# A gated cross-attention and expert kernel: another order of the set-up, scores straight from q, a folded gate, and heads gathered by transfers

## The reference

```python
x = x + tanh(g_xattn[0]) * xattn(layernorm(x), ctx, ctx, adj, mask, Wq, bq, Wk, bk, Wv, bv, Wo, bo)
x = x + tanh(g_ffn[0]) * moe(layernorm(x), gate_w, w1, b1, w2, b2)
# xattn: 16 heads of 16; softmax(Q K^T / 4 + adj, shut where mask == 0) V, then Wo and bo
# moe: 8 experts of 256 -> 1024 -> 256 with relu; each token goes to the one expert whose
#      gate logit (x @ gate_w.T) is largest, times its softmax probability
```

## Time and profile before

| | |
|---|---|
| three runs | 552.46, 554.51 (median), 555.67 us |
| profiled execution, span | 548.5 us (its own time is not given apart from the runs) |
| busy: PE, DVE, ACT, POOL | 526.3, 302.3, 309.1, 297.9 us |
| first score, last score | 27.35 us, 361.17 us |
| expert loop | from 413.99 us |
| DMA queue of SP | 46600 packets, 67.72 MB |

### The profile page before, as it was taken

How to read it: one execution, slowest core, us unless ns; L and a number is a source line. 1 busy time by engine, 2 the same in 40 slices (tenths; PEclk the granted TensorE clock), 3 DMA queues, 4 the chain that set the end, 5 groups by cost and what they waited for, 6 DMA issues and landing times. The chain is left out here.

```text
span 548.5 us, 13306 instructions
## 1 busy us (share of the span) xinstructions
PE 526.3 (96%) x4123; PEld 405.1 (74%) x4124; DVE 302.3 (55%) x923; ACT 309.1 (56%) x678; POOL 297.9 (54%) x424
## 2 busy tenths in 40 slices
PE   8999999989999999999999999888999999999997
PEld 5577667667666667666676666658899999999996
DVE  2776587976677887668885878845340211111111
ACT  4366678665678665778675676664332333333322
POOL 5346566665567575468574556555244444443451
PEclk9999999999999999999999999999999999999999
DMA  8633625400405510204520057499136665555570
GB/s 288 206 110 132 192 65 183 149 31 6 150 21 192 166 50 1 79 10 153 180 85 1 11 184 250 147 362 320 59 103 218 211 205 196 178 187 184 189 210 1
DMA packets 51489, 77.67 MB, mean 142 GB/s; under 512 B 9945, under 2 KB 34601, under 8 KB 51305
## 3 DMA queue, kind: packets, MB, share of 16 engines
q1 hardware_dynamic: 46600, 67.72, 37.0%
q0 software_dynamic: 4192, 8.73, 5.0%
q10 hardware_dynamic: 640, 0.52, 0.3%
HBM read 52.76 MB, written 8.35 MB: 111 GB/s over the span
## 5 line engine op out<-in xcount | busy, mean ns | idle before, releaser
L1588 DVE CUSTOM_DVE_ANT_0 prob<-bank,adjm 128x512 f32<-128x512 f32 x256 | 172.3, 688 | 70.6 <-issue 39.9
L1229 ACT ACTIVATE pt<-bank 128x512 f32<-128x512 f32 x256 | 152.1, 596 | 87.7 <-PE bank L951 81.2
L682 POOL TENSOR_SCALAR prob<-prob,negmax 128x512 f32<-128x512 f32 x190 | 132.0, 698 | 117.6 <-DVE negmax L1588 113.4
L951 PE MATMUL bank<-ident,prob 128*128 128x128 f32 x1024 | 154.8, 274 | 2.2 <-POOL prob L682 1.3
L951 PEld LDWEIGHTS bank<-ident,prob 128*128 128x128 f32 x1024 | 124.2, 141 | 39.7 <-issue 13.7
L1299 ACT ACTIVATE adjm<-bank,colsm 128x128 f32<-128x128 f32 x184 | 52.6, 368 | 105.0 <-PE bank L1127 80.0
L940 PE MATMUL bank<-w2s 128*128 128x512 bf16 x256 | 97.5, 381 | 8.5 <-DVE negmax L1588 5.7
L963 PE MATMUL bank<-pt,vals 128*32 128x256 f32 x1024 | 68.3, 385 | 0.9 <-DVE vals L1386 0.5
L1127 PEld LDWEIGHTS bank<-xT,pt 128*128 128x128 f32 x576 | 67.1, 192 | 0.9
L1127 PE MATMUL bank<-xT,pt 128*128 128x128 f32 x576 | 67.2, 275 | 0.0
L1137 PE MATMUL bank<-w2s,adjm 128*128 x288 | 65.1, 379 | 0.0
(11 more groups left out here) (195 smaller groups left out, 624.4 us busy)
## 6 DMA issues: line engine op xcount, KB each, us to landing
pt<-in_L_ffn_w SPq DMA_DIRECT2D x19, 1024.0 KB
w2s<-parts SPq DMA_DIRECT2D x96, 128.0 KB
w2s<-in_L_ffn_w SPq DMA_DIRECT2D x8, 1024.0 KB
maski<-in_mask_Bx1xSxS_ik SPq DMA_DIRECT2D x4, 1024.0 KB, 5.6
w2s<-parts SPq DMA_DIRECT2D x56, 64.0 KB, 2.1
xres<-in_x SPq DMA_DIRECT2D x18, 128.0 KB
x_d<-rows SPq DMA_DIRECT2D x18, 128.0 KB
xn_d<-rows SPq DMA_DIRECT2D x18, 128.0 KB
```

The lines of the kernel that those rows point to most:

```text
L682: po.tensor_scalar(prob[:, m], prob[:, m], -1.0, negmax[:, m:m + 1], ALU.mult, ALU.add).then_inc(s_shpool, 1)
L951: mm = pe.transpose(tr_bank[n % NTB][:, c * P:(c + 1) * P], prob[:, n % TILES % NB, c * P:(c + 1) * P], ident[:])
L1229: act.activation(pt[:, g % 2, :, j, q2 * P:(q2 + 1) * P], tr_bank[c % NTB][:].rearrange("p (c q) -> p c q", c=QT), ACT.Exp).then_inc(s_cac ...
L1588: ve.tensor_tensor_reduce(out=prob[:, m % NB], in0=sc_bank[m % NS][:], in1=adjm[:, qt], scale=-1.0, scalar=BIG, op0=ALU.add, op1=ALU.min, ...
```

## The change

1. Set-up. ScalarE issues Wk and the context; the sync queue x, Wq and small rows, and only one quarter of mask and bias first. k of the first half is projected before x is normalised. The eight tiles of head group 0 (both query tiles) of batch 0 are scored with float32 operands: k in `kf`, and `qm[:, j]`, a copy of q in which the rows of other heads are multiplied by zero (`own`). The group's stack is made later (tile 32 needs it).
2. Gate. Its weights are centred (mean taken off) and folded: Wo gets 8 more columns `Wo^T gate`, the bias 8 more elements, and a new use `gate x` gives x's part from the normalised x, multiplied back by `std`. A logit is then column 256 to 263 of the row, times 1/std, on GpSimd. Uses `normed` and `gate` are gone.
3. Heads. `heads` and `turn` are gone, except in the tail for the last half. Per half batch nine transfers gather `o_sb` into `oc` and the sums into 16 rows of `rc`; VectorE inverts these, four transfers spread them over `rs`, and VectorE multiplies `oc` by `rs` into `atT`.
4. Steps of many uses are moved by a few, and the load of b2 stands later on the sync queue.

```diff
-    ACT_SHIFTS = (3, 6)
+    ACT_SHIFTS = (2, 6)
...
+    PRO = ["Wk", "ctx0", "ctx1", "Wq", "small", "k0", "gate", "x0", "x1", "q0", "k1", "q1", "Wv", "Wo"]
+    DIRECT = 8
+    FILL = (10, 14, 8, 4)
...
+    TAIL_A = [(29, "out", 0), (33, "out", 1), (51, "rank", 0)]
+    USES = sorted([(10, "values", 0), (11, "values", 1)] + TAIL_A
+                  + [(12, "gate x", 0), (13, "next x", 0), (14, "next x", 1), (17, "next ctx", 0), (18, "next ctx", 1),
+                     (21, "next q", 0), (25, "next k", 0), (30, "next q", 1), (35, "next k", 1)]
+                  + [(55, "out", 2), (59, "out", 3)], key=lambda use: use[0])
...
+    SUMS_STEPS, SCALE_STEPS = ((15, 47), (13, 45)), ((20, 53), (18, 50))
...
+            def compact(par, qh):
+                for j in range(HG):
+                    to = slice(par * P // 2 + j * D, par * P // 2 + (j + 1) * D)
+                    sp.dma_start(oc[to], o_sb[j * VW:j * VW + D, par::2, qh]).then_inc(t_comp, 16)
+                if par == 1:
+                    sp.dma_start(rc, o_sb[D:P:VW, :, qh]).then_inc(t_sums, 16)
+            def spread(b, half):
+                sp.wait_ge(t_rc, b * 2 + half)
+                for a in range(NG):
+                    at = a % 2 * P // 2
+                    sp.dma_start(rs[at:at + P // 2, a // 2], rc[a:H:NG].rearrange("j (o q) -> j o q", o=1).to_broadcast(
+                        [HG, D, HALF])).then_inc(t_over, 16)
...
+                if b > 0:
+                    compact_old(b, 1)
+                    spread(b, 0)
...
+                compact_new(b, 0)
+                rows_out(b, (t + (NT - 2)) % NT, 0)
+                sp.wait_ge(s_parts, (b + 1) * 4 + 3)
+                stack_in(sp, par, 0, 0, 0, EC, range(PAIRS), s_stack)
+                rows_out(b, (t + (NT - 2)) % NT, 1)
+                compact_new(b, 1)
+                stack_in(sp, par, 0, 1, 0, EC, range(PAIRS), s_stack)
+                spread(b, 1)
                 rows_free(b, 0)
...
+                po.tensor_scalar(logit[:, (k + 2) % 4], rows[:, u, E:EX], rstd2[:, u:u + 1], None, ALU.mult
+                                 ).then_inc(t_logit, 1)
...
+                    po.tensor_copy(xres[:, u, E:], xg[:, k]).then_inc(t_xe, 1)
...
+                if what == "gate x":
                     o = bank_free(b, i)
+                    for c in range(EC):
+                        for t in range(QT):
+                            mm = pe.matmul(o[VW * t:VW * (t + 1), 0:P], gateT[:, c], xT[:, c, t * P:(t + 1) * P],
                                            start=c == 0, stop=c == EC - 1)
...
+                        mm = pe.matmul(o[:, 0:EX], atT[:, c, u * P:(u + 1) * P], woT[:, c], start=c == 0, stop=c == EC - 1)
...
+                if b == 0 and n < DIRECT:
+                    pe.matmul(sc_bank[m][:], qm[:, j, q2 * P:(q2 + 1) * P], kf, start=True, stop=True).then_inc(s_score, 1)
+                    return
...
+            def invert(b, half):
+                ve.wait_ge(t_sums, 16 * (b * 2 + half))
+                ve.reciprocal(rc, rc).then_inc(t_rc, 1)
+            def scale(b, half):
+                ve.wait_ge(t_comp, COMPACT * (b * 2 + half))
+                ve.wait_ge(t_over, SPREAD * (b * 2 + half))
+                ve.tensor_tensor(atT[:], oc[:], rs[:], ALU.mult).then_inc(t_atT, 1)
```

More of the change, by code:

```diff
@@ L105, in build @@
     USES = sorted([(10, "values", 0), (11, "values", 1)] + TAIL_A
[L106 to L110, removed]
@@ L474, in _ @@
             last = B - 1
-            tail_pair(last, last * QT - 2, 0, last * QT)
+            compact_old(last, 1)
+            spread(last, 0)
             sp.wait_ge(s_score, last * TILES)
@@ L620, in split @@
                 po.tensor_tensor(parts[:, t, 2, m], rest[:], parts[:, t, 1, m], ALU.subtract).then_inc(s_parts, 1)
+            po.wait_ge(s_adj0, 16)
+            mask(0, 0)
             po.wait_ge(s_adj, 16)
[L623 to L625 removed]
             def tail_rstd(b, k):
@@ L920, in tail_use @@
                 if what == "out":
-                    pe.wait_ge(t_atT, b * 4 + k + 1)
+                    pe.wait_ge(t_atT, b * 2 + (k // 2 + 1 if b < B else k + 1))
                     o = bank_free(b, i)
+                    if k == 0 and b < B:
+                        pe.wait_ge(s_xgs, b + 1)
+                        pe.transpose(o[:, EX:EX + P], xgs[:], ident[:])
                     for c in range(EC):
-                        mm = pe.matmul(o[:, 0:E], atT[:, u, c], wT[:, 3, c], start=c == 0, stop=c == EC - 1)
-                if what == "normed":
-                    pe.wait_ge(t_row, b * 4 + k + 1)
-                    o = bank_free(b, i)
-                    for c in range(EC):
-                        mm = pe.transpose(o[:, c * P:(c + 1) * P], rows[:, u, E + c * P:E + (c + 1) * P],
-                                          ident[:])
+                        mm = pe.matmul(o[:, 0:EX], atT[:, c, u * P:(u + 1) * P], woT[:, c], start=c == 0, stop=c == EC - 1)
                 mm.then_inc(s_m, 1)
@@ L989, in step @@
                 for i, what, k in at_step(uses, n):
-                    if what == "heads" and k == 2:
-                        pe.wait_ge(s_osb, b * GROUPS + (NG + 2))
                     if what == "values":
@@ L1056, in early_y @@
                     if s in (2, 3):
-                        pe.wait_ge(s_md[s % 2 ^ 1], tail_free(("gate", (0, 1)) if s == 2 else ("rank", 1)))
+                        pe.wait_ge(s_md[s % 2], tail_free(("out", 1) if s == 2 else ("rank", 1)))
                     pe.wait_ge(r_w2, 16 * X)
```

575 lines of the change are left out of this document (366 added, 209 removed).

## The result

| | changed kernel | kernel before |
|---|---|---|
| median | 558.21 us (557.34 to 560.43, 4 runs) | 553.71 us (552.46 to 555.67, 4 runs) |
| profiled execution, span | 557.93, 556.2 us | span 548.5 us |
| mean granted clock of the profiled execution | 0.984 | 0.998 |

The ratio is 1.0107, with a 95% interval from 1.0073 to 1.0141. The forecast was 537.5 us in a range of 526 to 551. Direction and range were both wrong.

A forecast was written before the change was run, and what follows sets the result against it. TensorE's own queue was taken to bound the batches (83 of 86 us). Batches 10.5 + 2.7, tail 1.25, set-up 4.5, less 2 for the sync queue, make 17 us: 554.5 - 17 = 537.5 us, range 526 to 551.

The forecast's parts named there:

- TensorE's work: Batches: removed transposes and gate products, less additions, free 4.15 us of TensorE a batch, 3.5 of it arriving in three batches.
- rival D: Batches: folded gate or masked copies cost TensorE what they replace, 3.4 us in all; counted within the forecast's 0.62.
- the reciprocal is then ready as well (65): Second half of a batch: reciprocal ready 65 us in, spread landed at 69.1, on time for step 53 by 1.4 us.
- 2 us for four batches: Sync queue: charge for thin margins of the new transfers over the four batches, 2 us (0 to 10).
- Rival C: Sync queue late: spread waits behind eight stack transfers, VectorE holds at step 53; batches lose 20.4 us, 558 us; chance 0.09.
- the set-up's 4.5 us: Set-up: first score at 16 instead of 27.35, tile 12 at 37.5 instead of 41.98, a gain of 4.5 us.
- about 10 us for eight tiles: Set-up: VectorE's time for eight tiles with k's and q's second halves and the next statistics among tiles 0 to 9.
- Rival A: Set-up gives nothing, tile 12 stays at 42 because ScalarE's issues and mask passes only move; 542 us; chance 0.16.
- the tail: After the last batch: four transposes (0.44) and eight gate products (0.81) leave TensorE, a gain of 1.25 us.
- the cover of VectorE's load: Batches: the long reciprocal's 1.8 us stall is hidden by three score banks, TensorE's lag on transposes and fillers.
- rival B: Batches: VectorE becomes what TensorE waits for, the gain of 13.2 us shrinks to 5, 545.5 us; chance 0.13.

The follow-up runs named there:

- e13: e10 with the second half's spread of the reciprocals issued by ScalarE at steps 47, 48, 49 and 51 instead of the sync queue; 541.57 us, ratio 0.9848.
- e11: e10 with the long reciprocal taken over the first 64 of 256 columns alone; 536.95 us, ratio 0.9777.
- e15: Changed kernel with the sync queue's edits alone, those of e2, e5 and e9; 547.39 us, ratio 0.9951.
- e2: Changed kernel with the sums in their own tile, and their transfer and the second compaction two stack transfers sooner, sums first; 553.74 us, ratio 1.0069.
- e8: e7 with the casts and splits of k's and q's second halves in the set-up on GpSimd instead of VectorE; 545.76 us, ratio 0.9937.
- e4: Changed kernel with the folded gate's bias at step 2 instead of 7 and the second x loaded ahead of the first stacks; 554.05 us, ratio 1.0075.
- e1: Changed kernel with the operands of the first eight scores rounded to bfloat16; 555.27 us, ratio 1.0084.
- e12: e10 with the operands of the first eight scores in bfloat16, as in e1; 540.66 us, ratio 0.9840.
- e10: e9 with the last batch's last shift (tile 63) on ScalarE instead of GpSimd; 540.52 us, ratio 0.9827.
- e14: e13 with each long reciprocal in two pieces of 128 columns, one step apart; 540.96 us, ratio 0.9833.
- e5: e2 with the spread of the reciprocals ahead of q's second-half stack transfers on the sync queue; 549.92 us, ratio 1.0007.
- e7: e6 with the two set-up edits of e4; 546.79 us, ratio 0.9951.
- e6: e5 with the statistics of x of the batch after next at steps 36, 42, 44 and 50; 550.12 us, ratio 1.0003.
- e9: e8 with the second pair's four compaction transfers issued by ScalarE at steps 42 to 45 and the second half's reciprocal at step 46; 542.84 us, ratio 0.9872.
- e3: Changed kernel with the statistics of x at steps 22, 26, 36 and 42 instead of 59, 62, 63 and 65; 559.63 us, ratio 1.0160.

## Why the prediction was wrong

**Right: TensorE's work.** Its busy time fell in the second batch although some of it was at half clock. Two batches of e13 at full clock have 79.9 and 79.6 us busy where the same batches before had 83.6 and 83.3: 3.7 us less, for the forecast's 4.15. They last 83.5 and 83.7 us, forecast 82.3 (85.8 - 3.5); 82.1 came only in e11, with three quarters of the reciprocal left out. The folded gate's 16 products take the queue from 45.90 to 46.48, 0.6 us for the estimated 0.75, so rival D was no part of it.

**Failed: the sync queue, "the reciprocal is then ready as well (65)".** This is the step that turned the sign. I worked out when the spread would land and compared it with step 53. I never wrote down when the sums would land beside step 47, where VectorE needs them first. By the prediction's own terms they were issued by 59.5 (57 + 2.5), landed by 61.6, and step 47 came at 63.2 (70.5 - 7.3): on time by 1.6 us. Measured from the batch's first score (117.6), the compaction began at 60.3 and not 57, behind eight stacks, which took 6.32 us, and two transfers of a row tile; four small issues cost 2.6 (0.65 each, forecast 0.5), and the sums landed at 64.9. Step 47 had been reached at 62.1. So the largest part of the error is the 3.3 us of the late start, and the wait stood at the reciprocal: 2.5, 2.8 and 2.4 us in the first three batches, then 1.74 for the instruction, and TensorE behind it. In the first halves, too, the product waited 1.1, 2.1 and 1.5 us for its spread where the forecast had 0.3. I charged 2 us for four batches. The edits of e15 were worth 1.56%, 8.6 us of 550.

Rival C had the right queue and the wrong place: VectorE was to hold at step 53, for the spread, and in the changed kernel it waits 0.1 to 0.3 us there. That leg shows only in e2, once the sums are on time (3.1, 3.0 and 2.2 us). Its 20.4 us also count four batches, while the last one has no stacks for the spread to stand behind, so by its own rule it is 15.3; and that its 558 is the measured 558.2 is luck, since the set-up and the tail, which it took as forecast, came out otherwise. At 9 in 100 it had too little all the same: its condition, "because the new issues cost 0.65 each", was the rate of the stack transfers in the earlier trace rows, the row nearest in kind.

**Failed: the set-up's 4.5 us.** Tile 0's mask came at 22.4 for a forecast of 19.4: the fourth masked copy, forecast for 17.4, took ScalarE to 20.3. What then took 5.6 us and 3.2 more was named in the working ("about 10 us for eight tiles") and priced too low. Eight tiles took 15.9 us: 5.5 for eight masks at 0.69, 4.4 for the parts of q's and k's second halves (0.75, 0.42 and 1.06 each), 2.4 for four statistics, 1.5 for a norm and the gate's bias, and 2 idle. Moving two of the splits away (e8) returned 2.0 us of it, and removing the bias's wait (e4) 1.6. Not seen at all: that the first eight scores are two float32 passes each (0.86 us of the queue in place of 0.22). It cost nothing that shows (e1, e12). And with e4's and e8's edits, tile 12's mask stands at 42.0 beside 42.5: half a microsecond for the whole new set-up. Rival A had this number for the mended kernel, but its reason, ScalarE's issues and mask passes, is not what the traces show: e8 moved VectorE's work and gained 2.0.

**Open: the tail.** I counted the TensorE work that leaves and not the constant beside it in the diff. With `LAST_ACT_SHIFTS` (60, 61) the last subtraction falls to GpSimd behind two indirect transfers, and TensorE waits 2.15 us for it. But the tail of one and the same code takes 49.0 to 54.5 us in the profiled executions of the changed kernel and e1 to e8, and the 2.3 us lost are one draw of these; of the kernel before there is one trace, with 52.3. Removing the wait (e10) didn't shorten the stretch. So neither the forecast's -1.25 nor the +2.3 is shown.

**Failed: the cover of VectorE's load.** 1.74 us for the long reciprocal, forecast 1.8 from the slope of the earlier trace rows; its row for the whole span:

```profile
L1601 DVE RECIPROCAL rest<-rest 16x256 f32<-16x256 f32 x7 | 12.2, 1738 | 7.6 <-DMA rest<-o_sb 7.6
```

The size was right and the cover was not: "the stall is hidden". Taking three quarters of it away gained 3.6 us in the median (e11), and cutting it in two gained nothing (e14). There are seven of them, since the last half goes the old way in the tail, and not eight, one for each half batch. Seven reciprocals of 535 ns instead of 1738 leave out 8.4 us, so some 4 in 10 of it reached the end. This is rival B's mechanism, VectorE as what TensorE waits for, at a smaller price than B's 8, and it is what the mended kernel still pays.

**The clock.** No step of the forecast had it. The changed kernel spent five stretches of 3.4 us at 0.50 of full speed, each behind a wait of TensorE of 2.1 to 2.8 us. A price can be read where the same code ran at both levels: the tail takes 50.5 and 50.3 us in e1 and e4 without such a stretch and 51.5 in e5, e7 and e8 with one, beside waits for GpSimd of 2.1 to 2.2 us in all five, so 1.0 to 1.2 us each. (Without a stretch and with shorter waits, 0.8 and 1.5 us, it takes 49.0 in e2 and 49.7 in e6.) An estimate from it, if the other stretches cost as much, is 5 to 6 us for the five, a part of the changed kernel's loss beside the waits themselves. The times point the same way: the two executions of e15 at a mean clock of 0.978 and 0.980 took 549.9 and 549.2 us, the eight at 0.986 to 0.988 took 546.1 to 548.3. It is not what e15 removed, since its clock is the changed kernel's.

**Where it went.** By ratio: the changed kernel 1.0107; sync queue -0.0156 (e15); last shift -0.0045 (e9 to e10); the rest of the way to e10's 0.9827, -0.0079, falls to the set-up's edits and the statistics, which were not timed on top of e15. Of these parts the first is shown (the intervals are far apart), the second is not (they overlap), and of the third e7's 0.5% over e6 is. As written, the gain of some 4 us a batch in TensorE's work was outweighed by waits, the larger part of them put there by the order of one queue, the rest by VectorE's work among the first tiles and its long reciprocal. e10 keeps the change and is 1.7% faster than the kernel before (0.9796 to 0.9859).

Open: whether GpSimd's splits alone hold tile 12 at 42.0 in e8 to e14; whether e11's gain is VectorE's load or the earlier reciprocals; and what the tail gains or loses.

## What to carry to other kernels

When a result travels by transfers between engines, list each consumer of each leg, and compare the landing with the first instruction that needs it, not with the last. Count the queue by the slowest issue in the trace, with what stands ahead of it. After mending one wait, look for the same microseconds at the next wait on the same queue (reciprocal, product, tile 64) before calling the theory wrong: e2, e5 and e9 each showed a part, and only together were they worth 1.6%. Constants that decide which engine does the last tile belong to the change as much as its functions do, even where, as here, no run shows what they cost. And before a stage of 50 us is said to have lost 2, look at the same code in the other traces: here it varied by 5.

## What was not expected of the hardware

In e1's rows above the wait of 1.11 us is followed by a score of 0.39 us, at full clock, and the wait of 2.07 us by one of 0.59, at half clock. Of the changed kernel's seven waits of 2.1 us and more ahead of the expert loop, five were followed by 3.4 us at that level and two, of 2.61 and 2.46 us, were not; the 0.91 us of the earlier trace rows and a wait of 1.90 in the kernel before, up to 377.19, were not either. The length of the wait doesn't tell the two apart: in the last batch one of 1.53 us, of the same code, has a stretch 1.2 to 1.7 us behind it in e1, e2, e4 and e6 and none in the changed kernel, e3, e5, e7 and e8. So in these traces a stretch at half clock may stand behind a wait of TensorE and need not, and in the tail it was worth 1.0 to 1.2 us. A reciprocal of 16x256 costs 1738 ns on VectorE although only 16 partitions hold data; with 936 ns for 128 columns (e14) and 535 for 64 (e11) that is 6.3 ns for each further column over some 0.13 us. ScalarE issued four transfers of 0.59 to 0.62 us among its exponentials (e10, 166.30 to 169.11) with no loss that shows.
